# Self attention fed from the norm's fp32r parts, the gate as column tiles, the choice in two pieces, and a shifted order of units

## The chip, the cores and the metric

The kernel runs on one core of one Trainium2 chip. The metric is the device time of one execution in microseconds (us). A core has TensorE (PE, with its weight loads PEld), VectorE (DVE), ScalarE (ACT), GpSimd (POOL) and a queue, SP, that issues transfers. Each engine takes its instructions strictly in the order of the program and meets the others at semaphores.

## What is computed

Eight sequences of 512 rows and 256 columns go through three layers, each followed by a layer norm of the sum with its input:

```python
x = norm(x + linear_attention(x))      # M=128: q, k, v; state = 0.99*state + 0.01*v k^T, out = state q; then Wo
x = norm(x + cross_attention(x, ctx))  # 16 heads of 16, softmax over 512 keys
# the last layer: self attention and a mixture of experts, side by side
qkv = (x @ W_qkv + b_qkv)              # 16 heads of 16
attn_out = softmax(q k^T / 4) v
gate = softmax(x @ W_gate + b_gate)    # 8 experts
combine = the two largest gate values at their experts, 0 elsewhere   # ties go to the lower expert
moe_out = sum_e combine[e] * (x @ W_experts[e] + b_experts[e])
x = norm(x + attn_out + moe_out)
```

## The kernel before

**Slots.** The two attentions of all sequences make 16 phases (C is the cross attention of a sequence, S its self attention; from the second sequence on they alternate), and a phase has 16 slots, each for 4 heads against 128 keys. A slot has two halves, t = 2s and t = 2s + 1. In each half TensorE makes two score tiles (`sc`, waiting for the exponential of the half before) and two tiles for the row maxima of six slots ahead (`mx`, of which VectorE reduces each to one column, `maxes`). The first half also holds the product with the values of the slot before (`op`). ScalarE takes one exponential of 1024 columns from each half (`probs`).

**Units.** All other TensorE work is cut into units: projections, transposes, the gate, the experts (`moe0` to `moe15` of each sequence, six fp32r matmuls of 512 columns each), the bias of the experts (`be0`, `be1`). Tables (`LIN...`, `MID_LONG`, `MID_SHORT`, `MOE_...`) give each unit a slot and a half, relative to the start of its cross phase; `MID_LONG` serves the sequences 1 to 6. TensorE runs the units of both halves of a slot at the end of its second half, those of half 0 first. ScalarE and VectorE take a unit's result out in the half after the one of the table, so a unit of half 0 is taken out in the second half of its own slot and one of half 1 in the first half of the next, behind that half's exponential on ScalarE and behind that half's maxima on VectorE. The results of units lie alternately in two PSUM banks (`ms`), and a unit waits until the last but one before it has been taken out (`wait_unit_out(pe, *ORDER[u - 2])`).

**Names.** Every fourth slot (2, 6, 10, ... of a phase) begins its units with `shift`, a transpose of the maxima, whose result VectorE copies (`shift_r`) for a transfer into `qs`, and ends them with `heads`, which transposes the output of four finished heads. `kc0, kc1, qc0, qc1` are the two halves of the cross attention's keys and queries, `k3c0, k3c1, q3c0, q3c1` those of self attention. ScalarE writes the high fp32r part of such a unit (`high`) and VectorE the low one (`low`), which is the rest; six transfers then stack them into `ks` or `qs`. `v3a, v3b` are self attention's values, `x0, x1`, `hT0, hT1` and `x2T0, x2T1` the transposes of a norm's output or of the heads, `v1, k1, s0, s1, s23, o1, y01, y23` units of the linear attention (its v is written to `lin`). The gate's steps are `gate` on TensorE, bias and maximum on VectorE, `g_exp` on ScalarE, `choose` on VectorE (normalise, compare each pair of experts, rank, `comb`). `comb` scales the experts' results, and `combT` transposes it for `be`.

**What is fp32 here.** k3, q3, v3 and the gate multiply `x2T`, a plain fp32 copy of the transposed norm, with fp32 weights; TensorE's record shows two matmuls for each fp32 one. The experts take `x2T` and their weights as a high and a low fp32r part and make three products (high by high, low by high, high by low). ScalarE writes `x2T` and `x2T_hi`, GpSimd subtracts them to `x2T_lo` (L978), which only the experts wait for. GpSimd also adds the experts' results to `x2` and runs the norm's root.

## Time and profile before

| | |
|---|---|
| median of 3 runs | 1332.31 us (1330.14 to 1338.65) |
| the profiled execution | 1330.05 us |
| its span, first to last instruction | 1328.3 us |
| mean granted TensorE clock | 0.986 of full speed |
| TensorE busy | 1240.0 us, 93% |
| VectorE busy | 904.8 us, 68% |
| ScalarE busy | 776.4 us, 58% |
| GpSimd busy | 364.9 us, 27% |

A share of busy time is an average over the whole span. What matters for a change is the chain that sets the pace at its place. In the rows below, a time in brackets is how long the engine had stood idle before the row, and what ended that.

### The profile page before, as it was taken

What the parts mean: (1) busy time and instruction counts of PE and PEld (TensorE: products, weight loads), DVE (VectorE), ACT (ScalarE), POOL (GpSimd) and SP (SyncE); (2) the same over time, 40 slices, a digit from 0 to 9 for tenths busy, and PEclk for the clock granted to TensorE, in tenths of its full rate; (3) what the DMA queues carried; (4) which work ended last, traced back from release to release, by engine and by line L of the source; (5) the groups of instructions that cost most, each with busy time, mean ns of one, the idle gap of its engine ahead of it and who ended that gap; (6) DMA issues with size and microseconds to landing.
All of it is one profiled execution on the core that took longest, in us unless ns stands there. A gap on an engine that the chain in (4) does not pass through costs nothing.

```text
span 1328.3 us, 19317 instructions
## 1 busy us (share of the span) xinstructions
PE 1240.0 (93%) x6648; PEld 593.1 (45%) x6648; DVE 904.8 (68%) x1809; ACT 776.4 (58%) x1087; POOL 364.9 (27%) x435
## 2 busy tenths in 40 slices
PE   7888989999999999999999999999999999998995
PEld 4433445444444444444444544444444444453442
DVE  5476776567776677767776677767677777767672
ACT  2254556666566655656656665666556566666564
POOL 2310013222521224311423216122252123322162
PEclk9889999999999999999999999999999999999999
DMA  6824134304443323334422243441243333213300
GB/s 233 137 41 69 38 49 65 49 14 68 65 65 49 48 54 46 65 49 64 66 50 50 32 80 49 65 65 27 41 65 49 50 48 45 55 16 49 49 19 16
DMA packets 49840, 74.85 MB, mean 56 GB/s; under 512 B 8520, under 2 KB 20048, under 8 KB 49488
## 3 DMA queue, kind: packets, MB, share of 16 engines
q1 hardware_dynamic: 48496, 72.70, 33.8%
q10 hardware_dynamic: 1248, 0.92, 0.4%
q8 instruction: 54, 0.88, 0.3%
q14 instruction: 42, 0.34, 0.1%
HBM read 18.02 MB, written 4.19 MB: 17 GB/s over the span
## 4 chain that ended last, share of the span: by engine, by line
PE 76%; DVE 10%; issue 5%; ACT 5%; DMA 2%; SPq 1%; POOL 0%; ACTq 0%; DVEq 0%; POOLq 0%
PE ms L412 37%; PE sc L412 14%; PE op L412 14%; PE mx L412 7%; DVE maxes L831 3%; PE ms L491 2%; PE ms L436 2%; DVE k_parts L746 2%; ACT k_parts L617 1%; ACT probs L677 1%; DMA qs<-q_parts 1%; ACT x L695 1%; DMA qs<-shift_r 1%; DVE ks L915 1%; SPq L362 1%
## 5 line engine op out<-in xcount | busy, mean ns | idle before, releaser
L831 DVE TENSOR_REDUCE maxes<-mx 128x1 f32<-128x512 f32 x1024 | 657.9, 684 | 342.2 <-PE mx L412 341.2
L677 ACT ACTIVATE probs<-sc 128x1024 f32<-128x1024 f32 x512 | 524.3, 1024 | 448.6 <-PE sc L412 443.9
L993 POOL TENSOR_TENSOR x<-x,moe 128x256 f32<-128x256 f32 x256 | 187.0, 730 | 630.5 <-ACT moe L670 605.3
L412 PE MATMUL op<-probs,v 128*32 128x512 f32 x2048 | 276.0, 611 | 2.2 <-ACT probs L677 1.1
L412 PE MATMUL sc<-qs,ks 50*128 50x512 f32 x1024 | 258.1, 501 | 10.7 <-ACT probs L677 6.8
L412 PEld LDWEIGHTS sc<-qs,ks 50*128 50x128 f32 x1024 | 95.9, 184 | 322.9 <-ACT probs L677 225.7
L412 PE MATMUL mx<-ks,qs 48*128 48x512 f32 x1024 | 208.5, 403 | 13.7 <-DVE maxes L831 13.4
L670 ACT ACTIVATE moe<-ms,comb 128x256 f32<-128x256 f32 x256 | 106.7, 472 | 18.4 <-PE ms L412 18.4
L412 PEld LDWEIGHTS mx<-ks,qs 48*128 48x128 f32 x1024 | 98.4, 188 | 21.6 <-DVE maxes L831 17.4
L412 PE MATMUL ms<-we_hi,x2T_hi 128*128 128x512 f32 x256 | 94.9, 451 | 6.3 <-DVE lin L765 3.5
L412 PEld LDWEIGHTS op<-probs,v 128*32 128x32 f32 x2048 | 40.4, 108 | 95.6 <-issue 94.2
L412 PE MATMUL ms<-we_lo,x2T_hi 128*128 128x512 f32 x256 | 80.6, 396 | 0.0
L412 PE MATMUL ms<-we_hi,x2T_lo 128*128 128x512 f32 x256 | 80.5, 396 | 0.0
L412 PE MATMUL ms<-x2T,w_wqkv 128*128 128x512 f32 x128 | 61.1, 602 | 4.2 <-DVE k_parts L746 4.1
L412 PEld LDWEIGHTS ms<-we_hi,x2T_hi 128*128 128x128 f32 x256 | 39.4, 189 | 38.2 <-issue 20.3
L412 PEld LDWEIGHTS ms<-we_lo,x2T_hi 128*128 128x128 f32 x256 | 48.4, 189 | 11.4
L412 PEld LDWEIGHTS ms<-we_hi,x2T_lo 128*128 128x128 f32 x256 | 48.1, 188 | 11.5
L948 POOL TENSOR_SCALAR var<-mv 128x4 f32<-128x4 f32 x24 | 5.6, 235 | 148.5 <-DVE mv L862 147.8
L491 PEld LDWEIGHTS ms<-w_ident,oT 128*128 128x128 f32 x256 | 30.5, 141 | 24.0 <-DVE shift_r L800 16.8
L491 PE MATMUL ms<-w_ident,oT 128*128 128x128 f32 x256 | 39.2, 276 | 1.1 <-ACT oT L616 0.8
L616 ACT ACTIVATE oT<-op 128x512 f32<-128x512 f32 x64 | 38.1, 595 | 1.2 <-PE op L412 1.2
L978 POOL TENSOR_TENSOR x2T_lo<-x2T,x2T_hi 128x512 fp32r<-128x512 f32 x16 | 20.4, 1272 | 65.0 <-ACT x2T_hi L616 65.0
(107 smaller groups left out, 1193.9 us busy)
## 6 DMA issues: line engine op xcount, KB each, us to landing
ks<-k_parts SPq DMA_DIRECT2D x192, 128.0 KB, 4.5
qs<-q_parts SPq DMA_DIRECT2D x189, 128.0 KB, 5.6
xT_s<-in_xT SPq DMA_DIRECT2D x8, 512.0 KB, 4.8
x_s<-in_x SPq DMA_DIRECT2D x8, 512.0 KB, 4.4
ctxT_s<-in_ctxT SPq DMA_DIRECT2D x8, 512.0 KB, 3.9
out<-x SPq DMA_DIRECT2D x7, 512.0 KB, 2.9
qs<-shift_r SPq DMA_DIRECT2D x128, 8.0 KB
probs<-in_we SPq DMA_DIRECT2D x1, 1024.0 KB, 7.7
```

The lines of the kernel that those rows point to most:

```text
L362: sp.dma_start(dst[at:at + HD, e % RING, :, :], part[name][64 * side:64 * side + 64, which[r], :]).then_inc(stack_in[name], 16)
L412: return nc.tensor.matmul(dst, lhsT, rhs, start=first, stop=last, skip_group_check=True)
L436: last = nc.tensor.transpose(bank[:, t * P:(t + 1) * P], src[:, t, c * P:(c + 1) * P], ident[:])
L491: last = nc.tensor.transpose(bank[:, t * P:t * P + P], oT[:, t * P:t * P + P], ident[:])
L616: return nc.scalar.activation(dst, src, ACT.Copy)
L617: return nc.scalar.activation(dst, src, ACT.Identity, bias=bias, scale=1.0)
L670: nc.scalar.activation(moe[:, k % 2, j * D:j * D + D], bank[:, j * D:j * D + D], ACT.Copy, scale=comb[:, t, e:e + 1]).then_inc(moe_out, 1)
L677: nc.scalar.activation(probs[:, (2 * s + h) % 3, :, :], sc[:], ACT.Exp).then_inc(exp_out, 1)
L746: nc.vector.scalar_tensor_tensor(out=part[name][:, 1, :].bitcast(F32R), in0=unit_bank((task, n)), scalar=bias[:, c:c + 1], in1=part[name][ ...
L831: nc.vector.tensor_reduce(maxes[:, g % 2, at:at + 1], mx[:, i % 3, :], AX_X, ALU.max).then_inc(max_out, 1)
L978: nc.gpsimd.tensor_tensor(x2T_part[1][:, c, :].bitcast(F32R), x2T[:, c, :], x2T_part[0][:, c, :], ALU.subtract).then_inc(x2_low, 1)
L993: nc.gpsimd.tensor_tensor(x2[:, n % 2, t, :], x2[:, n % 2, t, :], moe[:, k % 2, j * D:j * D + D], ALU.add).then_inc(acc, 1)
```

## The change

**Self attention from parts.** `wqkv3` is no longer kept in fp32. It is loaded in two pieces into tiles that are free at the start (`heads` and half of `moe`), scaled there, and cut into `w3_part` (high on ScalarE, low on GpSimd) behind the same cut of the experts' weights. k3 and q3 become six fp32r matmuls of 512 columns, v3a and v3b twelve of 256. The fp32 copy `x2T` is gone: ScalarE writes only `x2T_hi`, and VectorE takes `x2T_lo` straight from PSUM, which then frees the bank.

**The gate as column tiles.** The gate's weight, padded to 32 columns, is now the stationary operand. Sixteen matmuls, each two records, write the four row blocks of 128 to four groups of 32 partitions; both parts of x2T pass through in fp32. ScalarE copies the result, and a new unit `gateT` transposes it back.

**The choice in two pieces.** `choose` stops after the two comparisons, and `choose_end` has the other four operations, half a slot later.

**The order.** The units of keys and values in the slots with `shift` (kc0, kc1, k3c0, k3c1, v3a) move from half 1 to half 0. hT0, hT1, x0 and x1 move about a slot later, be0 and be1 one to three slots, and moe0 to moe12 of most sequences one to two.

```diff
-LIN = {"q1": (-36, 1), "k1": (-35, 1), "v1": (-34, 1), "s0": (-27, 0), "s1": (-25, 0), "s23": (-24, 0),
-       "o1": (-23, 1), "y01": (-21, 0), "y23": (-20, 0), "x0": (-17, 0), "x1": (-16, 0), "kc0": (-14, 1),
+LIN = {"q1": (-36, 1), "k1": (-33, 1), "v1": (-32, 1), "s0": (-27, 0), "s1": (-25, 0), "s23": (-24, 0),
+       "o1": (-23, 1), "y01": (-21, 0), "y23": (-20, 0), "x0": (-16, 0), "x1": (-15, 0), "kc0": (-14, 0),
...
-MID_LONG = {"hT0": (19, 0), "hT1": (20, 0), "cy0": (21, 1), "cy1": (22, 1), "x2T0": (27, 0), "x2T1": (28, 0),
-            "gate": (29, 0), "combT": (32, 0), "be0": (33, 0), "be1": (36, 0), "k3c0": (34, 1), "q3c0": (35, 1),
+MID_LONG = {"hT0": (20, 0), "hT1": (20, 1), "cy0": (21, 1), "cy1": (22, 1), "x2T0": (27, 0), "x2T1": (28, 0),
+            "gate": (29, 0), "gateT": (31, 0), "combT": (33, 1), "be0": (36, 0), "be1": (37, 0), "k3c0": (34, 0), "q3c0": (35, 1),
...
-            "apply23": (26, 0), "g_exp": (30, 0), "choose": (30, 1)}
+            "apply23": (26, 0), "g_exp": (32, 0), "choose": (32, 1), "choose_end": (33, 0)}
...
+            def project_parts(dst, wt, src, cols):
+
+                for m, (i, j) in enumerate(((0, 0), (1, 0), (0, 1))):
+                    for c in range(DC):
+                        last = mm(dst, wt[j][:, c, cols].bitcast(F32R), src[i][:, c, :].bitcast(F32R),
+                                  m == 0 and c == 0, m == 2 and c == DC - 1)
+                return last
...
+            def project_part_rows(bank, width, src, wt, cols, blocks):
+
+                for b, t in enumerate(blocks):
+                    for m, (i, j) in enumerate(((0, 0), (1, 0), (0, 1))):
+                        for c in range(DC):
+                            last = mm(bank[:, b * width:(b + 1) * width], src[i][:, c, t * P:(t + 1) * P].bitcast(F32R),
+                                      wt[j][:, c, cols].bitcast(F32R), m == 0 and c == 0, m == 2 and c == DC - 1)
+                return last
...
+            def gate_blocks(bank, src, wt):
+
+                for i in range(2):
+                    for c in range(DC):
+                        for t in range(TB):
+                            last = mm(bank[GATE_W * t:GATE_W * t + GATE_W, 0:P], wt[:, c, :], src[i][:, c, t * P:t * P + P],
+                                      i == 0 and c == 0, i == 1 and c == DC - 1)
+                return last
...
+                elif task == "gateT":
+                    wait_unit_out(pe, "gate", n)
+                    last = nc.tensor.transpose(bank[:, 0:P], gateT, ident[:])
...
-                    copy(x2T[:, c, :], bank)
-                    copy(x2T_part[0][:, c, :].bitcast(F32R), bank).then_inc(done, 1)
+                    copy(x2T_part[0][:, int(task[3]), :].bitcast(F32R), bank).then_inc(x2_high, 1)
+                elif task == "gate":
+                    wait_unit(act, task, n)
+                    copy(gateT, bank[:, 0:P]).then_inc(done, 1)
...
                     for c in range(DC):
                         copy(we_part[0][:, c, :].bitcast(F32R), we_stage[c]).then_inc(we_cut, 1)
+                    for k in range(2):
+                        copy(w3_part[0][:, :, W3_COLS[k]].bitcast(F32R), w3_stage[k]).then_inc(w3_cut, 1)
...
+                elif task in ("x2T0", "x2T1"):
+                    c = int(task[3])
+                    dve.wait_ge(x2_high, DC * n + c + 1)
+                    nc.vector.tensor_tensor(x2T_part[1][:, c, :].bitcast(F32R), bank, x2T_part[0][:, c, :],
+                                            ALU.subtract).then_inc(x2_low, 1)
...
-                elif task in ("x2_low0", "x2_low1"):
-                    c = int(task[-1])
-                    wait_unit_out(pool, f"x2T{c}", n)
-                    nc.gpsimd.tensor_tensor(x2T_part[1][:, c, :].bitcast(F32R), x2T[:, c, :], x2T_part[0][:, c, :],
-                                            ALU.subtract).then_inc(x2_low, 1)
...
+                    pool.wait_ge(w3_cut, 2)
+                    for k in range(2):
+                        nc.gpsimd.tensor_tensor(w3_part[1][:, :, W3_COLS[k]].bitcast(F32R), w3_stage[k],
+                                                w3_part[0][:, :, W3_COLS[k]], ALU.subtract).then_inc(w3_cut, 1)
```

**TensorE, from `heads` of the slot with k3c0 to q3c0 of the next slot, sequence 2.** The `w_ident,oT` row is `heads`, `x2T,w_wqkv` is q3c0. Before:

```order
L491 MATMUL ms<-w_ident,oT 128x128 x4
L412 MATMUL sc<-qs,ks 128x512 x2
L412 MATMUL mx<-ks,qs 128x512 x2
L412 MATMUL op<-probs,v_1 32x512 x4
L412 MATMUL sc<-qs,ks 128x512 x2
L412 MATMUL mx<-ks,qs 128x512 x2
L412 MATMUL ms<-x2T,w_wqkv 128x512 x2
```

And in the changed kernel, where the `we_` rows are moe1 and the `w_hi`, `w_lo` rows q3c0:

```order
L527 MATMUL ms<-w_ident,oT 128x128 x4
L422 MATMUL sc<-qs,ks 128x512 x2
L422 MATMUL mx<-ks,qs 128x512 x2
L422 MATMUL op<-probs,v_1 32x512 x4
L422 MATMUL sc<-qs,ks 128x512 x2
L422 MATMUL mx<-ks,qs 128x512 x2
L422 MATMUL ms<-we_hi,x2T_hi 128x512 x2
L422 MATMUL ms<-we_hi,x2T_lo 128x512 x2
L422 MATMUL ms<-we_lo,x2T_hi 128x512 x2
L422 MATMUL ms<-x2T_hi,w_hi 128x512 x2
L422 MATMUL ms<-x2T_lo,w_hi 128x512 x2
L422 MATMUL ms<-x2T_hi,w_lo 128x512 x2
```

One unit, moe1, now stands between the scores of the slot and q3c0, and q3c0 is six records instead of four (each fp32 matmul makes two).

**VectorE, the maxima around k3c0, the same place.** `shift_r` is the copy of `shift`, `k_parts` the low part of k3c0, the last two rows take out `heads`. Before:

```order
L800 COPY shift_r<-ms 32x128
L831 TENSOR_REDUCE maxes<-mx 128x1 x2
L746 SCALAR_TENSOR_TENSOR k_parts<-ms,w_bk,k_parts 128x512
L807 RECIPROCAL rsum<-ms 128x16
L809 TENSOR_TENSOR heads<-ms,rsum 128x4x64
```

In the changed kernel:

```order
L848 COPY shift_r<-ms 32x128
L794 SCALAR_TENSOR_TENSOR k_parts<-ms,w_bk,k_parts 128x512
L884 TENSOR_REDUCE maxes<-mx 128x1 x2
L855 RECIPROCAL rsum<-ms 128x16
L857 TENSOR_TENSOR heads<-ms,rsum 128x4x64
```

The low part goes ahead of the next slot's first two maxima.

**VectorE, the choice of sequence 2.** `lin` is the taking out of v1, `comb` the end of the choice. Before:

```order
L800 COPY shift_r<-ms 32x128
L885 TENSOR_REDUCE g_s<-g_e 128x4
L887 RECIPROCAL g_s<-g_s 128x4
L889 TENSOR_TENSOR g_p<-g_e,g_s 128x32
L896 TENSOR_TENSOR above<-g_p 128x256
L897 TENSOR_TENSOR tied<-g_p 128x256
L900 TENSOR_TENSOR tied<-tied,w_earlier 128x256
L904 TENSOR_TENSOR above<-above,tied 128x256
L906 TENSOR_REDUCE rank<-above 128x32
L910 SCALAR_TENSOR_TENSOR comb<-rank,g_p 128x32
L831 TENSOR_REDUCE maxes<-mx 128x1 x2
L765 TENSOR_TENSOR lin<-ms,w_bv 128x512
```

In the changed kernel:

```order
L938 TENSOR_REDUCE g_s<-g_e 128x4
L940 RECIPROCAL g_s<-g_s 128x4
L942 TENSOR_TENSOR g_p<-g_e,g_s 128x32
L949 TENSOR_TENSOR above<-g_p 128x256
L950 TENSOR_TENSOR tied<-g_p 128x256
L884 TENSOR_REDUCE maxes<-mx 128x1 x2
L813 TENSOR_TENSOR lin<-ms,w_bv 128x512
L959 TENSOR_TENSOR tied<-tied,w_earlier 128x256
L963 TENSOR_TENSOR above<-above,tied 128x256
L965 TENSOR_REDUCE rank<-above 128x32
L969 SCALAR_TENSOR_TENSOR comb<-rank,g_p 128x32
```

Two maxima and the taking out of v1 now stand inside the choice, and no longer behind it; the whole lies two slots later (in slot 80 of the kernel in place of 78, with its end in slot 81).

## Rows read from the trace of the kernel before

**Rows 1.** Busy time by stretch: us, PE, PEld, DVE, ACT, POOL, PEclk, DMA, GB/s.

```profile
404.20:561.10 156.90, 150.84 (x829) 72.54 (x828) 111.28 (x226) 96.03 (x135) 45.03 (x54) 1.00 0.34 55
```

**Rows 2.** Waits of TensorE, 404.2 to 561.1 us (total, times, longest).

```profile
PE ms L436 <- DVE heads L809: 1.3, 1, 1.3
PE ms L412 <- DVE k_parts L746: 1.2, 2, 0.6
PE ms L436 <- ACT x L695: 1.0, 1, 1.0
PE ms L412 <- DVE lin L765: 0.7, 1, 0.7
PE ms L436 <- DVE k_parts L746: 0.6, 1, 0.6
PE mx L412 <- DVE maxes L831: 0.6, 1, 0.6
...
PE ms L412 <- DVE v L752: 0.3, 1, 0.3
```

**Rows 3.** Timeline of TensorE, 480.4 to 490 us (start us, us, ...).

```profile
480.46 0.40 PE L412 MATMUL mx<-ks,qs 48*128 48x512 f32 x2
...
480.78 1.06 PE L412 MATMUL op<-probs,v 128*32 128x512 f32 x8
...
481.78 0.50 PE L412 MATMUL sc<-qs,ks 50*128 50x512 f32 x2
...
482.12 0.39 PE L412 MATMUL mx<-ks,qs 48*128 48x512 f32 x2
...
482.44 1.13 PE L412 MATMUL ms<-w_be,o1T 8*128 8x256 f32 x4
...
483.49 0.73 PE L412 MATMUL ms<-we_hi,x2T_hi 128*128 128x512 f32 x2
...
485.09 0.50 PE L412 MATMUL sc<-qs,ks 50*128 50x512 f32 x2
...
486.76 0.50 PE L412 MATMUL sc<-qs,ks 50*128 50x512 f32 x2
...
487.55 1.88 PE L412 MATMUL ms<-x2T,w_wqkv 128*128 128x512 f32 x4
...
489.27 0.60 PE L491 MATMUL ms<-w_ident,oT 128*128 128x128 f32 x4
...
489.80 0.50 PE L412 MATMUL sc<-qs,ks 50*128 50x512 f32 x2
```

**Rows 4.** Timeline of all engines, 487 to 494.7 us, from `shift` to q3c0.

```profile
487.53 1.29 DVE L831 TENSOR_REDUCE maxes<-mx 128x1 f32<-128x512 f32 x2 [0.38 <-PE mx L412]
...
488.74 0.27 DVE L800 COPY shift_r<-ms 32x128 f32<-32x128 f32 x1
...
491.26 0.68 ACT L617 ACTIVATE k_parts<-ms,w_bk 128x512 fp32r<-128x512 f32 x1
...
491.98 0.75 DVE L746 SCALAR_TENSOR_TENSOR k_parts<-ms,w_bk,k_parts 128x512 fp32r<-128x512 f32 x1
...
492.78 1.98 PE L412 MATMUL ms<-x2T,w_wqkv 128*128 128x512 f32 x4 [0.59 <-DVE k_parts L746]
```

**Rows 5.** The gate in the timeline of TensorE, at 461.85 us.

```profile
461.85 1.95 PE L412 MATMUL ms<-w_wg,x2T 128*128 128x8 f32 x16
```

**Rows 6.** Instructions by line: x count, busy us, mean ns of one, idle before, releasers.

```profile
L412 PEld LDWEIGHTS ms<-we_hi,x2T_hi 128*128 128x128 f32 x256 | 39.4, 189 | 38.2 <-issue 20.3 <-DVE lin L765 5.0 <-ACT moe L670 4.8
...
L412 PE MATMUL ms<-w_wg,x2T 128*128 128x8 f32 x128 | 15.6, 257 | 0.0
```

**Rows 7.** A transfer in the chain that ended last, in order of time.

```profile
190.44 7.88 DMA qs<-q_parts
```

**Rows 8.** Timeline of the start, ScalarE and TensorE.

```profile
49.36 1.90 ACT L616 ACTIVATE we_hi<-x 128x2048 fp32r<-128x2048 f32 x1
...
52.56 1.12 PE L412 MATMUL ms<-x1T 128*128 128x512 f32 x2
```

More of the change, by code:

```diff
@@ L79 @@
+MOE_FIRST = [(26, 1), (27, 0), (28, 0), (29, 0), (30, 1), (31, 0), (32, 1), (33, 0), (33, 1), (36, 1), (37, 0),
+             (38, 0), (39, 0), (40, 0), (41, 0), (41, 1)]
+MOE_LAST_BUT_ONE = [(33, 1), (35, 0)] + [(s, 1) for s in (36, 37, 40, 41)] + [(43, 0), (44, 0)] + \
                    [(s, 1) for s in (44, 45, 46, 47, 48, 49)] + [(52, 0), (52, 1)]
[L80 removed]
+MOE_LAST = [(26, 1), (28, 0), (30, 1)] + [(s, 1) for s in range(32, 45)]
@@ L81 @@
 MOE_ENTRIES = TB * E // 2 + 2
 UNITS_LIN = ("q1", "k1", "v1", "s0", "s1", "s23", "o1", "y01", "y23", "x0", "x1", "kc0", "qc0", "cv0", "cv1", "kc1", "qc1")
-UNITS_MID = ("hT0", "hT1", "cy0", "cy1", "x2T0", "x2T1", "k3c0", "q3c0", "gate", "k3c1", "q3c1", "v3a", "v3b",
+UNITS_MID = ("hT0", "hT1", "cy0", "cy1", "x2T0", "x2T1", "k3c0", "q3c0", "gate", "gateT", "k3c1", "q3c1", "v3a", "v3b",
              "combT", "be0", "be1")
@@ L151, in own_signal @@
 def own_signal(task):
-    return task in SPLITS or task in ("be0", "be1", "shift", "heads", "gate") or task.startswith("moe")
+    return task in SPLITS or task in ("be0", "be1", "shift", "heads", "gateT", "x2T0", "x2T1") or task.startswith("moe")
 TAKEN = {unit: sum(not own_signal(ORDER[v][0]) for v in range(u % 2, u + 1, 2)) for u, unit in enumerate(ORDER)}
@@ L182, in plan_others @@
         halves["pool"][lin_at("x1_bias", n)].append(("x1_bias", 1, n))
-        for c in range(DC):
-            halves["pool"][mid_at(f"x2T{c}", n) + 2].append((f"x2_low{c}", 1, n))
         if n + 1 < B:
@@ L219, in sem @@
             return ctx.enter_context(nc.semaphore(name))
-        W = {name: sb("w_" + name, list(ap.shape)) for name, ap in w.items() if name != "we"}
+        W = {name: sb("w_" + name, list(ap.shape)) for name, ap in w.items() if name not in STAGED}
         ident = W["ident"]
@@ L236, in decoder @@
         combT = o1T[0:E, :]
+        gateT = sb("gateT", [P, P])[:]
         x1 = sb("x1", [P, TB, D])
@@ L270, in decoder @@
         we_part = (sb("we_hi", [P, DC, E * D]), sb("we_lo", [P, DC, E * D]))
+        w3_part = (sb("w3_hi", [P, DC, 3 * D]), sb("w3_lo", [P, DC, 3 * D]))
+        w3_stage = (heads[:].rearrange("p n d -> p (n d)").rearrange("p (c d) -> p c d", c=DC),
+                    moe[:, 0, :].rearrange("p (c d) -> p c d", c=DC))
+        W3_COLS = (slice(0, 2 * D), slice(2 * D, 3 * D))
         we_stage = (probs[:].rearrange("p s h t -> p (s h t)")[:, 0:E * D],
@@ L299, in decoder @@
         G_STEPS = 12
-        LATE = tuple(n for n in w if n not in FIRST + EARLY and n != "we")
+        LATE = tuple(n for n in w if n not in FIRST + EARLY + STAGED)
         block = ctx.enter_context(nc.Block())
@@ L506, in unit @@
                     wait_unit_out(pe, "x2T1", n)
+                    if n == 0:
+                        pe.wait_ge(w3_cut, 4)
                     at = (D if task[0] == "k" else 0) + c * P
-                    last = project(bank, W["wqkv3"], x2T, slice(at, at + P))
+                    last = project_parts(bank, w3_part, x2T_part, slice(at, at + P))
                 elif task in ("v3a", "v3b"):
@@ L512, in unit @@
                     wait_unit_out(pe, "x2T1", n)
-                    last = project_rows(bank, D, x2T, W["wqkv3"], slice(2 * D, 3 * D), (2 * h, 2 * h + 1))
+                    if n == 0:
+                        pe.wait_ge(w3_cut, 4)
+                    last = project_part_rows(bank, D, x2T_part, w3_part, slice(2 * D, 3 * D), (2 * h, 2 * h + 1))
                 elif task == "gate":
@@ L516, in unit @@
                     wait_unit_out(pe, "x2T1", n)
-                    last = project_rows(bank, E, x2T, W["wg"], slice(0, E), range(TB))
+                    last = gate_blocks(bank, x2T_part, W["wg"])
+                elif task == "gateT":
+                    wait_unit_out(pe, "gate", n)
+                    last = nc.tensor.transpose(bank[:, 0:P], gateT, ident[:])
                 elif task == "combT":
```

46 lines of the change are left out of this document (28 added, 18 removed), and 6 rows, old and new, of tables (LIN, MID_LONG, MID_SHORT).

## Prediction

> **What bounds the kernel now.** I read the busy time by stretch first. From about 243 us to 1181 us the kernel repeats a pattern of 32 slots; one such period takes 156.90 us [rows 1], TensorE is busy for 150.84 us of it, VectorE for 111.28, ScalarE for 96.03, and the granted clock is the full one (2.4 GHz). So TensorE sets the pace there, and two things can shorten a period: less work on TensorE, and fewer waits of it. The waits of TensorE in the same period come to 6.0 us [rows 2], each a unit that waits for its bank or its input. The timeline then gives the price list [rows 3]. The second scores of a slot start 1.67 us after the first (485.09 to 486.76), whatever the slot holds, since they wait for the exponential. After the second scores, 0.66 us pass until the first unit (481.78 to 482.44). A bias unit takes 1.05 us (to 483.49). An expert unit of six fp32r matmuls takes 1.60 us to the next scores (485.09), of which about 0.19 us is a tail that every such slot has: two experts in one slot cost 1.41 us each, 0.235 per matmul. k3c0, two fp32 matmuls in four records, takes 1.72 us (487.55 to 489.27), and `heads` with the tail 0.53. So the second half costs 0.85 us plus its units: 1.41 for an expert, 1.72 for a k3, q3 or v3 unit, about 0.35 for four small transposes.
>
> **k3 and q3.** Six fp32r matmuls of 512 columns are an expert unit's shape: 1.72 becomes 1.41, 0.31 less. Per period there are four. q3c0 and q3c1 give it all. k3c0 and k3c1 stand between `shift` and `heads`, and `heads` uses the bank of `shift`, which VectorE frees at 489.01 [rows 4], behind two maxima; the transposes then start no earlier than about 489.1 in place of 489.27 [rows 3]. There I count 0.15. Sum: 2 × 0.31 + 2 × 0.15 = 0.9 us.
>
> **v3a and v3b.** Twelve fp32r matmuls of 256 columns, each with its own load of 128 columns. The kernel has no such sequence. Bounds: the old gate is 16 records of 8 columns whose loads alone pace it, 0.113 us each (1.95 us less the last one's own 0.26, over 15) [rows 5, 6]; a weight load by itself lasts 0.189 [rows 6]. Twelve at 0.113 are 1.36 us, twelve at 0.189 are 2.27; now it is 1.72. The loads run ahead of the matmuls in the gate, and half of an expert's stream (0.235 / 2) is also 0.118, so I take a value near the low end, 0.125 or 1.50 us: 0.22 less for v3b, 0.15 for v3a (the bank of `shift` again). Sum 0.4 us; at the upper end it would be a loss of 1.1 per period. The Trainium skill ("TensorE: Matmul & The Clock Gate", "LDWEIGHTS (loading the stationary operand)") has a load take its columns over 1.2 GHz, 107 ns for 128: by that the unit is 1.28 us, and the kernel some 3 us faster than my sum; the row of 0.113 stands against so low a value.
>
> **The gate.** Its 16 records take 1.95 us to the end of the last and 1.69 to its start [rows 5, 6], which is what the slot pays beside the tail. Now there are 32 records of 128 columns in four column groups. `op` is the row nearest: eight records of 512 columns in four groups, started within 0.5 us of each other and finished within 1.06 [rows 3], so four run at a time. A quarter of the columns gives 0.107 us for each four, 0.85 in all; if issue or loads pace them as in the old gate, up to 1.7. I take 1.1, and 0.15 for `gateT`: 0.45 less, with 0 as the other bound. One rule speaks against this form: the Trainium skill ("TensorEngine Tiling (Array Packing)", "Key Properties") says that a change of tiling mode drains TensorE. The kernel changes mode in each slot, and `mx` to `op` takes 0.32 us, as does `mx` to a full-width unit [rows 3]; no drain is seen. By the rule, two more changes per sequence might cost some 0.3 us, 2.5 in all.
>
> **The waits.** This is the large term. After a unit with parts, the low part lies behind ScalarE's next exponential and VectorE's next maxima: k3c0 ends at 489.27, its high part is written from 491.26, the low part ends at 492.73, and q3c0 waits 0.59 us [rows 4]. In half 0 both are done before the next slot's maxima, and moe1 now stands before q3c0. Of the waits [rows 2] I expect these to go: hT0 on `heads` (1.3; hT0 is a slot later), q3c0 and y01 on `k_parts` (1.2), x0 on the norm (1.0; a slot later), x2T0 on `k_parts` (0.6), one on v (0.3). In all 4.4; the view starts a wait at the modelled end of the matmul before, and for q3c0 the slot has lost 0.64 where it shows 0.59, so I count 4.8. The choice holds TensorE twice in a row, at `mx` (0.6) and at moe0, which waits for v1 behind the choice (0.7). In pieces it holds nothing at `mx`, but combT now waits for its end: in that slot VectorE has two maxima (1.3), v1's 0.7 and four operations of 1.6, which end some 0.7 us after TensorE could start combT. Gain 1.3 − 0.7 = 0.6.
>
> **What it costs.** VectorE takes over x2T_lo, 2 × 0.75 us per period (the low part of k3c0 is the same form [rows 4]), on an engine that has 45 us to spare; it lies behind the maxima of its half, a slot ahead of the gate. ScalarE loses a copy. A slot left with only `shift` and `heads` cannot fall below 1.6 us in its second half: 0.3 lost. A leading low part ends at about 5.85 us after its slot's start, where the next maxima are ready at about 5.5; the scores after them need the first maximum only 0.8 us later. That slack hides it.
>
> **The sum.** Per period 0.9 + 0.4 + 0.45 + 4.8 + 0.6 − 0.3 = 6.85 us. From 243 to 1032 us there are five periods: 34 us. From 1032 to 1181 us the same units save, but no next sequence's linear attention waits: 4 us. At both ends I count nothing: before 243 us and after 1181 us the first maxima of self attention wait for the stacking of q3c0 (a transfer stands 7.88 us on the chain at 190.44 [rows 7]); what is saved before it is mostly waited for, and one or two experts move from in front of that wait to behind it. The start loses: ScalarE cuts 2048 weights per row in 1.90 us, now 1536 more (1.5 us), ahead of the copies of q1 and k1, for which s0 starts at 52.56 with nothing to spare [rows 8]: 1.3 us. In all 34 + 4 − 1.3 = 36.7, from the profiled 1330.05 us to 1293. That execution lies 2 us below the median of the runs, so 1294 for a median.
>
> **Rivals.** (a) The sum as above, chance 0.60: 1281 to 1304. (b) v3's loads are not hidden: twelve at 0.189, 1.5 us per period more than I count, in eight sequences 12 us: 1306; chance 0.08. For it: nothing here shows a 256-column fp32r matmul. Against: the old gate's loads. (c) The waits only move. Each unit waits for the unit two before it, and there is hardly a slot in which something isn't moved; if half of the 4.8 comes back at other units, six times, 14 us: 1308; chance 0.2. For it: x2T_lo and the low parts are one after another on VectorE. (d) The change of order brings nothing, so that only the cheaper units count: 1.75 × 6 − 1.3 = 9 us, 1321; chance 0.07. (e) The other side: VectorE stands in its order behind the high part. It waits from the copy of `shift` (about 4.0 us into the slot) to the end of ScalarE's part (5.1), and meanwhile no maximum is taken. There are about 30 leading units in the repeating part. If a high part came later by 0.5 us or more, `mx` would wait; it decides at 0.8 us each (24 us, then the change is worth less than 1%), and from 1.7 us each, 50 us, it is slower: 1345. Against it: VectorE is idle for 45 us a period, and only one part comes per slot. Chance 0.05, half of it above 1345.
>
> **The numbers.** 1294, the median by (a). The range goes from the low ends of v3 and the gate with a few more waits gone, 1279, to (c) and a little beyond, 1313. About 1% (13 us) is what a measurement of this kernel can tell from no change. Faster by more means below 1319: (a), (b), (c) and half of (d), 0.92; within 1%: 0.055; slower 0.025.
>
> **What the profile will show.** A stretch of 32 slots at about 150 us in place of 156.90; k3 units of six records 0.235 us apart; v3 records 0.12 to 0.13 apart; the gate within 1.3 us; no wait on `k_parts` or on the norm's x; a wait of about 0.7 at combT; the start later by about 1.3 us. I am wrong if v3's records are spaced over 0.15 us, if `mx` waits for maxima in the slot after a leading unit, or if new waits at moe units add up to over 2 us per period.

## The result and the profile after

| | before | after |
|---|---|---|
| median of the runs | 1331.22 us (1327.26 to 1338.65, 4 runs) | 1293.26 us (1290.36 to 1295.98, 4 runs) |
| ratio | | 0.9706, 95% interval 0.9673 to 0.9738 |
| the profiled execution | 1330.05 us | 1295.17 us |
| its span | 1328.3 us | 1293.4 us |
| mean granted TensorE clock | 0.986 | 0.981 |
| TensorE busy | 1240.0 us | 1224.4 us, 95% |
| VectorE busy | 904.8 us | 911.8 us, 70% |
| ScalarE busy | 776.4 us | 776.9 us, 60% |
| GpSimd busy | 364.9 us | 348.4 us, 27% |

The kernel is 2.9% faster: 38.0 us between the medians, 34.9 us between the two profiled executions. I locate the gain by the starts of the first scores of a slot. Below, a slot's "second half" is the time from its second scores to the next slot's first ones.

| us from slot to slot | slot 0 begins | 0 to 34 | 34 to 66 | 66 to 98 | 98 to 194 | 194 to 226 | 226 to 255 |
|---|---|---|---|---|---|---|---|
| before | 73.15 | 170.08 | 160.95 | 156.93 | 470.80 | 149.00 | 132.18 |
| after | 73.69 | 172.79 | 154.26 | 150.27 | 450.71 | 144.56 | 131.89 |
| gain | -0.54 | -2.71 | 6.69 | 6.66 | 20.09 | 4.44 | 0.29 |

So five stretches of 32 slots gain 6.7 us each, the stretch with no further linear attention gains 4.4, and 3.3 us are lost before slot 34. The busy times of one period of the changed kernel, columns as in [rows 1]:

```profile
400.74:551.01 150.27, 148.77 (x862) 73.77 (x861) 112.07 (x229) 96.00 (x134) 42.49 (x52) 1.00 0.34 58
```

Against [rows 1] TensorE does 2.1 us less and idles 1.5 us where it idled 6.1: two thirds of a period's gain is time in which TensorE stood waiting. The view of waits in the same period has these left for TensorE (total, times, longest):

```profile
PE sc L422 <- ACT probs L721: 0.5, 2, 0.2
...
PE ms L422 <- DVE x1b L835: 0.3, 1, 0.3
PE ms L564 <- DVE comb L969: 0.3, 1, 0.3
...
PE ms L422 <- ACT o1T L659: 0.2, 1, 0.2
```

Every row of [rows 2] is gone: there is no wait on `k_parts`, on the norm's `x`, on `heads`, on `lin` or on `maxes`. The next fence is the timeline of the changed kernel in that period, in the form of [rows 3, 4]: the gate in slot 77, the end of the choice and combT in slot 81, k3c0 in slot 82, q3c0 in slot 83, v3a in slot 86.

```profile
458.04 0.64 PE L422 MATMUL ms<-x2T_hi,w_wg 128*32 128x128 f32 x16
458.50 0.62 PE L422 MATMUL ms<-x2T_lo,w_wg 128*32 128x128 f32 x16
459.05 0.51 PE L422 MATMUL sc<-qs,ks 50*128 50x512 f32 x2
...
475.25 0.19 DVE L969 SCALAR_TENSOR_TENSOR comb<-rank,g_p 128x32 f32<-128x32 f32 x1
...
475.59 0.60 PE L564 MATMUL ms<-w_ident,comb 128*8 128x128 f32 x4 [0.28 <-DVE comb L969]
...
478.92 0.73 PE L422 MATMUL ms<-x2T_hi,w_hi 128*128 128x512 f32 x2 [0.16 <-ACT o1T L659]
479.49 0.63 PE L422 MATMUL ms<-x2T_lo,w_hi 128*128 128x512 f32 x2
...
479.96 0.63 PE L422 MATMUL ms<-x2T_hi,w_lo 128*128 128x512 f32 x2
...
480.68 0.69 ACT L660 ACTIVATE k_parts<-ms,w_bk 128x512 fp32r<-128x512 f32 x1 [0.91 <-PE ms L422]
...
481.40 0.75 DVE L794 SCALAR_TENSOR_TENSOR k_parts<-ms,w_bk,k_parts 128x512 fp32r<-128x512 f32 x1 [1.38 <-ACT k_parts L660]
...
482.07 1.28 DVE L884 TENSOR_REDUCE maxes<-mx 128x1 f32<-128x512 f32 x2
...
484.79 0.63 PE L422 MATMUL ms<-x2T_hi,w_hi 128*128 128x512 f32 x2
...
499.80 0.40 PE L422 MATMUL ms<-w_hi,x2T_lo 128*128 128x256 f32 x2
500.04 0.40 PE L422 MATMUL ms<-w_lo,x2T_hi 128*128 128x256 f32 x2
```

The gate's 32 records and the tail of the slot lie between 458.04 and 459.05. k3c0's second and third pair start 0.47 us apart, 0.235 a record, and v3a's pairs of 256 columns 0.24 apart, 0.12 a record. Before, the low part of k3c0 ended at 492.73, 2.93 us into the next slot, which began at 489.80 [rows 3, 4]; now it ends at 482.15, 1.20 us into the next slot, which begins at 480.95. q3c0 at 484.79 has no bracket: it waits for nothing. VectorE pays for it: it stands 1.38 us behind the high part.

**Where the 2.7 us before slot 34 went.** Slot 22 of the first sequence takes 9.05 us in place of 6.96. Its k3c0 needs both low parts of x2T, and the second one stands behind a maximum on VectorE. The timeline of the changed kernel at that place:

```profile
179.63 1.27 DVE L884 TENSOR_REDUCE maxes<-mx 128x1 f32<-128x512 f32 x2
...
180.83 0.68 DVE L864 TENSOR_TENSOR x2T_lo<-ms,x2T_hi 128x512 fp32r<-128x512 f32 x1
181.43 1.27 DVE L884 TENSOR_REDUCE maxes<-mx 128x1 f32<-128x512 f32 x2
181.76 0.71 PE L422 MATMUL ms<-x2T_hi,w_hi 128*128 128x512 f32 x2 [0.68 <-DVE x2T_lo L864]
...
182.84 1.06 PE L422 MATMUL ms<-x2T_hi,w_lo 128*128 128x512 f32 x2
```

and its busy times by stretch there, with the granted clock third from the end:

```profile
180.00:184.00 4.00, 2.96 (x10) 2.13 (x11) 2.89 (x6) 0.89 (x2) 0.00 (x0) 0.83 0.02 4
184.00:188.00 4.00, 4.00 (x22) 2.41 (x21) 1.27 (x2) 1.43 (x2) 0.00 (x0) 0.74 0.24 68
```

After the wait the same pair of records lasts 1.06 us in place of 0.63, with the granted clock at 0.74 in the mean, between the two levels. The slot has two waits that the kernel before doesn't have there: 0.54 us of `mx` for the maxima, then 0.68 of k3c0. In the repeating part a whole slot lies between x2T and the gate, and nothing waits for `x2T_lo`.

How much of the 2.1 us in slot 22 is the wait, and how much the clock? Eight of the kernels below also have the changed kernel's first sequence. Five of them (parts_only, no_lead, early_transposes, q_leads, comb_later) show slot 22 at 7.95 us, with the same two waits and the full clock; in two (parts_late_comb, w3_later) it takes 9.05 as here; in one_choice the clock fell a slot earlier. So the waits are worth about 1.0 us against the slot of before (more, since its units have become cheaper), and the fall of the clock behind them 1.1 us, which comes in some executions only. The rest of the stretch: slots 23 to 26, in the last of which the first maxima of self attention wait for the stacking of q3c0, take 20.5 us in place of 18.7, again 0.7 of it where the clock fell (slot 26: 8.85 us, 8.1 to 8.2 in those five kernels); slots 1 and 2 are 1.7 longer and slot 12 is 1.5 shorter, which the same kernels show either way; and the cheaper units from slot 27 on give 1.2 back.

### The profile page after: what moved, and what is told of

It is laid out like the page before. It is cut to its first block, busy times and chain, and to the rows that moved or that the text cites. A ratio compares the mean times of both kernels' runs of the same rounds, so it can differ in the third digit from the quotient of the medians.

```text
span 1293.4 us, 19863 instructions
## 1 busy us (share of the span) xinstructions
PE 1224.4 (95%) x6912; PEld 603.1 (47%) x6912; DVE 911.8 (70%) x1825; ACT 776.9 (60%) x1081; POOL 348.4 (27%) x421
## 4 chain that ended last, share of the span: by engine, by line
PE 78%; DVE 9%; ACT 5%; issue 4%; DMA 2%; SPq 1%; POOL 0%; ACTq 0%; DVEq 0%
PE ms L422 36%; PE op L422 15%; PE sc L422 15%; PE mx L422 8%; DVE maxes L884 4%; ACT probs L721 2%; PE ms L527 2%; DMA qs<-q_parts 2%; PE ms L472 1%; ACT moe L714 1%; DVE ks L974 1%; SPq L370 1%; PE ms L522 1%; DVE x1b L835 1%; DMA qs<-shift_r 1%
## 5 line engine op out<-in xcount | busy, mean ns | idle before, releaser
L794 DVE SCALAR_TENSOR_TENSOR k_parts<-ms,w_bk,k_parts 128x512 fp32r<-128x512 f32 x32 | 24.0, 751 | 39.2 <-ACT k_parts L660 38.7
L660 ACT ACTIVATE k_parts<-ms,w_bk 128x512 fp32r<-128x512 f32 x32 | 22.0, 687 | 28.8 <-PE ms L422 28.8
```

Source lines behind the costliest of these rows:

```text
L660: return nc.scalar.activation(dst, src, ACT.Identity, bias=bias, scale=1.0)
L794: nc.vector.scalar_tensor_tensor(out=part[name][:, 1, :].bitcast(F32R), in0=unit_bank((task, n)), scalar=bias[:, c:c + 1], in1=part[name][ ...
```

## Experiments

### One half of the change at a time

**order_only** has before's arithmetic with the new tables, without gateT and with the choice in one piece:

```diff
-"gate": (29, 0), "combT": (32, 0), "be0": (33, 0), "be1": (36, 0), "k3c0": (34, 1)
+"gate": (29, 0), "combT": (33, 1), "be0": (36, 0), "be1": (37, 0), "k3c0": (34, 0)
...
-"g_exp": (30, 0), "choose": (30, 1)}
+"g_exp": (32, 0), "choose": (32, 1)}
```

> The kernel before with the changed kernel's order of units and nothing else: fp32 k3, q3, v3 and gate (no gateT, the choice in one piece, at the changed place). Theory A (most of the gain is waits that the order removes): per period of 32 slots 5.1 us of the 6.7 that the changed kernel gains, so a period near 151.8 us and a whole of about 1303 us. Theory B (the waits vanish only because the units became shorter, and the order adds little): a period above 154.5 us, 1317 us or more.

Measured: 1323.51 us (1318.77 to 1327.62), ratio 0.9926 (0.9899 to 0.9952). The period came out near the expected one, 152.86 for 151.8 us, but the whole is 20 us above the 1303 expected: what the periods give is largely lost at both ends (see below). **parts_only** is its counterpart: the new arithmetic with before's tables for the sequences 1 to 6, where gateT and the choice had to find a place:

```diff
-"gate": (29, 0)
+"gate": (29, 0), "gateT": (30, 0)
...
-"g_exp": (30, 0), "choose": (30, 1)}
+"g_exp": (31, 0), "choose": (31, 1), "choose_end": (31, 1)}
```

> The changed kernel with the old order for sequences 1 to 6 (LIN, LIN_THIRD, MID_LONG and the experts' tables of before; gateT at slot 30, g_exp and the whole choice at slot 31). Theory A: 1.7 us per period from the cheaper units, less what the later choice costs at moe0, so 155 to 156.5 us a period and 1322 to 1328 us. Theory B: most of the gain is here, below 1310 us.

Measured: 1333.31 us (1328.11 to 1336.76), ratio 1.0003 (0.9975 to 1.0031): no gain, where 5 to 11 us were expected. The starts of slots for these two, and for the experiments below:

| us | slot 0 begins | 0 to 34 | 34 to 66 | 66 to 98 | 98 to 130 | 194 to 226 | 226 to 255 |
|---|---|---|---|---|---|---|---|
| before | 73.15 | 170.08 | 160.95 | 156.93 | 156.93 | 149.00 | 132.18 |
| after | 73.69 | 172.79 | 154.26 | 150.27 | 150.22 | 144.56 | 131.89 |
| order_only | 71.16 | 177.22 | 156.84 | 152.86 | 152.86 | 151.22 | 137.22 |
| parts_only | 72.93 | 170.85 | 163.89 | 158.50 | 156.95 | 146.81 | 132.55 |
| parts_late_comb | 73.05 | 172.70 | 162.40 | 156.94 | 156.93 | 148.36 | 133.34 |
| no_lead | 73.98 | 170.95 | 157.09 | 153.11 | 153.09 | 147.46 | 133.93 |
| early_transposes | 78.34 | 169.81 | 155.71 | 151.70 | 151.69 | 145.35 | 134.08 |
| one_choice | 75.30 | 169.98 | 154.84 | 150.90 | 150.90 | 147.49 | 131.82 |
| q_leads | 72.81 | 170.89 | 156.83 | 151.00 | 150.94 | 145.74 | 133.52 |
| comb_later | 72.52 | 170.98 | 154.98 | 150.96 | 151.03 | 145.31 | 132.59 |
| x2T1_leads | 73.84 | 170.66 | 154.20 | 150.26 | 150.23 | 144.63 | 133.42 |
| w3_later | 71.44 | 171.99 | 154.24 | 150.20 | 150.19 | 144.66 | 133.04 |
| order_mid | 74.59 | 170.30 | 157.02 | 152.86 | 154.42 | 150.21 | 134.69 |

Slot 0 begins between 71 and 75 us in kernels that are the same up to there (once at 78), so differences of that column alone tell nothing.

A period is 156.93 with neither half, 152.86 with the order alone (152.2 if the choice in one piece costs what it does below), 156.95 with the parts alone, 150.24 with both. The two halves don't add up: with the order in place the parts give 2.6 us, without it nothing. parts_only shows why. Its cheaper units are there: against before the second halves of slots 77, 82, 83, 86, 87, 90 and 91 are shorter by 0.78, 0.15, 0.32, 0.15, 0.32, 0.15 and 0.31 us. Slot 79, where moe0 waited for v1, is shorter by 1.20. But with gateT between `shift` and v1 in slot 78, v1 falls to the bank of `shift`, which VectorE hasn't emptied, and the choice comes in one piece of nine operations. TensorE in its timeline, slots 78 and 80:

```profile
470.70 0.27 PE L559 MATMUL ms<-w_ident,gateT 128*128 128x128 f32 x1
472.22 2.05 PE L421 MATMUL ms<-w_wv,xT_s 128*128 128x128 f32 x16 [1.24 <-DVE shift_r L847]
...
480.62 0.51 PE L421 MATMUL sc<-qs,ks 50*128 50x512 f32 x2
482.70 0.76 PE L421 MATMUL mx<-ks,qs 48*128 48x512 f32 x2 [1.57 <-DVE maxes L883]
483.39 1.01 PE L563 MATMUL ms<-w_ident,comb 128*8 128x128 f32 x4
484.06 1.20 PE L421 MATMUL ms<-we_hi,x2T_hi 128*128 128x512 f32 x2
```

Slot 78 is 1.62 longer than before's, slot 80 longer by 1.84 at full clock and by 3.36 in this period, where the clock fell behind the wait (the pair of experts lasts 1.20 in place of 0.73 us). **parts_late_comb** moves combT and be0 out of that wait's way:

```diff
-"combT": (32, 0), "be0": (33, 0), "be1": (36, 0)
+"combT": (33, 0), "be0": (35, 0), "be1": (36, 0)
```

> The kernel of parts_only (cheaper units, the old order), in which combT waited 3.4 us for the choice, with combT a slot later and be0 two slots later in the long sequences, so that this wait has room. If the cheaper units are worth what the sum took (1.75 us per period) and moe0's old wait of 1.2 is gone as it was there, less 1.3 for gateT in a slot with shift: about 155 us per period and 1318 us. If the order, not the units, carries the gain, this stays far above 1293; if the two only work together for another reason, it stays near 1333.

Measured: 1336.28 us (1333.36 to 1345.56), ratio 1.0039 (1.0018 to 1.0059). The expectation was wrong: the wait only passed from combT to moe1 (slot 80 alone with moe1 has a second half of 4.13 us, where one expert needs 2.27), and slot 78 is as it was. The loss sits at the choice and at gateT's place, not at combT. Other places for gateT or a choice in two pieces within the old order were not tried, so that the cheaper units bring nothing is shown for these places only; k3, q3 and v3 gave their full 1.4 us a period even here.

### The moves one by one, taken back from the changed kernel

**no_lead** puts the units with `shift` back behind the next maxima:

```diff
-"kc0": (-14, 0)
+"kc0": (-14, 1)
...
-"kc1": (-6, 0)
+"kc1": (-6, 1)
...
-"k3c0": (34, 0)
+"k3c0": (34, 1)
...
-"v3a": (38, 0)
+"v3a": (38, 1)
...
-"k3c1": (42, 0)
+"k3c1": (42, 1)
```

> The changed kernel with kc0, kc1, k3c0, k3c1 and v3a of the repeating part back in half 1; TensorE's order is the same, only the taking out comes half a slot later. Theory A: the next unit waits again for the low part: 0.64 at qc0, about 0.5 at x2T0, 0.6 at moe1, 0.4 at s1, 0.65 at y01, 2.8 us per period, 15 us in all, about 1308 us. Rival (VectorE standing behind the high part costs as much as the lead brings): within 3 us of the changed kernel's 1293.

Measured: 1313.20 us (1312.33 to 1315.06), ratio 0.9853 (0.9791 to 0.9915). A period is 2.84 us longer, at the five units that follow a part: slots 67, 75, 83, 87 and 91 have 3.24, 3.87, 4.31, 3.32 and 3.80 us in place of 2.58, 3.33, 3.67, 2.94 and 3.13. In its timeline the wait of [rows 4] is back, now at moe1, which stands ahead of q3c0:

```profile
486.32 0.73 PE L422 MATMUL ms<-we_hi,x2T_hi 128*128 128x512 f32 x2 [0.58 <-DVE k_parts L794]
```

So the expert before q3c0 does not cover the wait, it takes it over: it is the lead that removes it. (The lead without that expert was not run.) The rest lies outside the periods, 2.9 us of it from slot 194 to 226, where the same units follow each other.

**early_transposes** puts hT0, hT1, x0 and x1 a slot earlier:

```diff
-"x0": (-16, 0), "x1": (-15, 0)
+"x0": (-17, 0), "x1": (-16, 0)
...
-"hT0": (20, 0), "hT1": (20, 1)
+"hT0": (19, 0), "hT1": (20, 0)
```

> The changed kernel with x0, x1 and hT0, hT1 a slot earlier again (as before), everything else as changed. Theory A: x0 waits about 1.0 us for the norm and hT0 about 1.3 us for heads, once per period each: 2.3 us less what the slots they leave then save (nothing), 13 us in all, about 1306 us. Rival (the faster slots have moved the norm and the heads early enough): no wait, 1293 us.

Measured: 1304.01 us (1300.41 to 1307.10), ratio 0.9779 (0.9725 to 0.9833). A period is 1.46 us longer, not 2.3. Slot 67 with hT0 and qc0 has 3.78 and slot 68 gives 0.44 back: 0.76 for the wait on `heads`. Slot 95 has 3.72 and slot 97 gives 0.39 back: 0.75 for the wait on `x`. Its view of waits tells why this is less than the 2.3 of [rows 2]:

```profile
PE ms L472 <- ACT x L739: 1.0, 1, 1.0
PE ms L472 <- DVE heads L857: 0.8, 1, 0.8
```

The wait on `heads` had been 1.3; the lead of kc0 has already taken 0.5 of it. The one on `x` is as long as before, but in the changed kernel the next slot's first scores wait 0.2 us for their exponential there, which is a part of the same time.

**one_choice** joins the choice again in the place of its first piece:

```diff
-"choose_end": (33, 0)}
+"choose_end": (32, 1)}
```

> The changed kernel with the whole choice in one piece at slot 80 (second half). Theory A (the two pieces let two maxima and v1 pass between them): mx of slot 81 then waits about 1.0 us behind the choice and combT no longer waits for its end but for v1: 0.6 to 1.0 us more per period, 1296 to 1299 us. Rival (the place of the choice, not its cut, is what counts): 1293.

Measured: 1302.22 us (1300.01 to 1303.77), ratio 0.9775 (0.9746 to 0.9804). A period is 0.65 us longer, all of it in slot 81 (3.81 in place of 3.15), as expected: 3.2 us in five periods. The stretch from slot 194 to 226 loses 2.9 more, all of it in slot 209 (8.01 in place of 5.11), where the choice stands for the last sequence but one: `mx` waits 1.87 us there for the maxima in place of 0.27, and the granted clock falls behind it. The profiled execution (1300.01) is 4.8 us above the changed kernel's; the 9 us between the medians go beyond that since it was the fastest of its four runs and the changed kernel's profiled one was 1.9 above its median. So the 6.1 us of these six stretches are what the cut accounts for.

### Going further

**q_leads** lets the queries' units lead too:

```diff
-"qc0": (-13, 1)
+"qc0": (-13, 0)
...
-"qc1": (-5, 1)
+"qc1": (-5, 0)
...
-"q3c0": (35, 1)
+"q3c0": (35, 0)
...
-"q3c1": (43, 1)
+"q3c1": (43, 0)
```

> The changed kernel with qc0, qc1, q3c0 and q3c1 of the repeating part in half 0 as well. No heads unit follows them, so their high part ends only 0.7 us after the slot, and VectorE stands in its order behind it. Theory (the lead pays only where heads covers it): the next maxima come about 0.7 us late, mx and the exponential each wait 0.1 to 0.2 us, four times per period, against 0.25 won at q1 and 0.3 at moe11: 0.2 to 0.7 us more per period, 1294 to 1297. Rival (a lead always pays): 0.5 us less per period, 1290.

Measured: 1300.22 us (1299.45 to 1301.84), ratio 0.9762 (0.9729 to 0.9795). Worse by 0.7 us a period, the upper end of what was expected (the total is above it): nothing waits for these parts early, while the slots after them (68, 76, 84) wait 0.16 for their exponential, which now stands behind the high part on ScalarE, and slot 84 loses 0.23 more. A lead pays only where the next unit needs the bank.

**comb_later** takes combT away from the end of the choice, where the changed kernel still waits:

```diff
-"combT": (33, 1)
+"combT": (35, 0)
```

> The changed kernel with combT two slots later for the sequences 1 to 6: from the end of slot 81 to slot 83 (sequence 2), ahead of moe1. In the changed kernel combT waits for the end of the choice (about 0.7 us in slot 81), and its copy on ScalarE then stands ahead of slot 82's parts (0.28 us more there than its units cost). If these two are losses of their own, slot 81's second half falls from 3.15 to about 2.3 us, slot 82's from 3.17 to 2.9, slot 83's rises from 3.67 to 4.0 for the transposes: 0.8 us per period, 5 to 6 periods, 1288 to 1289 us. If the slots are held by something else at the same time (the expert's results, the bank), the waits reappear at moe0, k3c0 or be0 and the time stays at 1293.

Measured: 1298.35 us (1297.09 to 1301.30), ratio 0.9732 (0.9703 to 0.9762): slower by 5 us, where 4 us less were expected. The second half of slot 81 did fall, to 2.27 us, and that of slot 82 to 2.89; a period grew by 0.7 all the same. The timeline shows both new waits:

```profile
473.05 1.28 DVE L884 TENSOR_REDUCE maxes<-mx 128x1 f32<-128x512 f32 x2
...
473.88 0.49 PE L422 MATMUL mx<-ks,qs 48*128 48x512 f32 x2 [0.44 <-DVE maxes L884]
...
482.01 0.60 PE L564 MATMUL ms<-w_ident,comb 128*8 128x128 f32 x4
...
483.10 0.73 PE L422 MATMUL ms<-x2T_hi,w_hi 128*128 128x512 f32 x2 [0.49 <-ACT moe L714]
```

With slot 81 shorter, VectorE is not through with the choice and the maxima behind it when slot 82's `mx` is due, and its first half has 2.37 us in place of 1.66. In slot 83, q3c0 now wants the bank of moe1, which ScalarE has just begun to empty: 4.85 us in place of 3.67, of which the transposes are some 0.35. combT's wait was cover for VectorE.

**x2T1_leads** moves x2T1 of the first and last sequence half a slot ahead of k3c0's slot:

```diff
-"x2T1": (21, 1)
+"x2T1": (21, 0)
```

> The changed kernel with x2T1 in half 0 for sequences 0 and 7, the two in which k3c0 comes in the next slot. In the changed kernel k3c0 of sequence 0 waits 0.68 us more by the trace for x2T_lo on VectorE (181.76), the granted clock falls for the rest of the slot, and the slot takes 9.05 us in place of 6.96. Theory (the late low part causes both): k3c0 does not wait, the clock stays, that slot is back at about 6.7 us, and q3c0's stack and the maxima of self attention come 2 us earlier: 1290 to 1291. Rival (the fall of the clock has another cause, or the gain is lost again at the transfer): 1293.

Measured: 1294.72 us (1294.24 to 1296.34), ratio 0.9722 (0.9698 to 0.9747): no difference from the changed kernel, where 2 to 3 us less were expected. k3c0 no longer waits, but slot 22 takes 7.63 us and not the 6.7 expected: VectorE now has both low parts ahead of its maxima, and `mx` waits for these.

```profile
179.20 1.27 DVE L864 TENSOR_TENSOR x2T_lo<-ms,x2T_hi 128x512 fp32r<-128x512 f32 x2
...
180.40 2.55 DVE L884 TENSOR_REDUCE maxes<-mx 128x1 f32<-128x512 f32 x4
181.13 0.49 PE L422 MATMUL mx<-ks,qs 48*128 48x512 f32 x2 [1.07 <-DVE maxes L884]
```

So it is VectorE's work in this slot, not the place of one low part, that costs the time; the move is worth 0.3 us against the 7.95 of the kernels in which the clock doesn't fall. Slots 0 to 34 take 170.66, but kernels with x2T1 in its old place come to 170.9 as well: 1.9 us of the 2.7 lost there are of the execution, not of the kernel.

**w3_later** cuts the self attention's weights two slots later, behind the copies of q1 and k1:

```diff
                         copy(we_part[0][:, c, :].bitcast(F32R), we_stage[c]).then_inc(we_cut, 1)
+                if t == 2 * -10:
                     for k in range(2):
                         copy(w3_part[0][:, :, W3_COLS[k]].bitcast(F32R), w3_stage[k]).then_inc(w3_cut, 1)
```

> The changed kernel with the high cut of the self attention's weights two slots later, so that ScalarE writes the copies of q1 and k1 before it. If the cut is what delays the start, the first scores of slot 0 come about 0.5 us earlier (72.9 to 73.2 us in place of 73.69) and the time is 1292.5; if the start does not hang on it, or the cut now delays a later copy by as much, it stays at 1293.

Measured: 1293.21 us (1292.23 to 1295.77), ratio 0.9697 (0.9667 to 0.9726). The cause is confirmed in the timeline. After first:

```profile
46.38 0.69 ACT L660 ACTIVATE q_parts<-ms,bq2s 128x512 fp32r<-128x512 f32 x1 [3.86 <-DMA qs<-q_parts]
...
50.56 1.04 ACT L659 ACTIVATE w_hi<-heads 128x1024 fp32r<-128x1024 f32 x1
51.51 0.62 ACT L659 ACTIVATE w_hi<-moe 128x512 fp32r<-128x512 f32 x1
52.03 0.67 ACT L660 ACTIVATE x1T<-ms,w_bq 128x512 f32<-128x512 f32 x1
...
53.43 2.04 PE L422 MATMUL ms<-x1T 128*128 128x512 f32 x2 [1.39 <-ACT x1T L660]
```

and w3_later:

```profile
46.57 0.69 ACT L660 ACTIVATE q_parts<-ms,bq2s 128x512 fp32r<-128x512 f32 x1 [3.87 <-DMA qs<-q_parts]
...
50.76 0.68 ACT L660 ACTIVATE x1T<-ms,w_bq 128x512 f32<-128x512 f32 x1
...
51.90 1.06 ACT L659 ACTIVATE w_hi<-heads 128x1024 fp32r<-128x1024 f32 x1
...
52.16 1.12 PE L422 MATMUL ms<-x1T 128*128 128x512 f32 x2
```

s0 follows `q_parts` after 7.05 us with the cut ahead and after 5.59 with it behind: 1.46 us. That is within the scatter of the whole kernel, and neither version is measurably the better (1292.5 us were expected).

### The ends of order_only

order_only loses 7.1 us before slot 34, 2.2 from slot 194 to 226 and 5.0 after slot 226. **order_mid** gives the first and last sequence their old gate, choice and experts back:

```diff
-             "k3c0": (22, 0), "q3c0": (22, 1), "gate": (23, 0), "k3c1": (27, 1), "q3c1": (28, 1), "v3a": (29, 1),
+             "k3c0": (22, 0), "q3c0": (22, 1), "gate": (24, 0), "k3c1": (27, 1), "q3c1": (28, 1), "v3a": (29, 1),
...
-MOE_LAST = [(26, 1), (28, 0), (30, 1)] + [(s, 1) for s in range(32, 45)]
+MOE_LAST = [(s, 1) for s in (25, 26, 30)] + [(s, 1) for s in range(32, 45)]
```

> The new order with the arithmetic of before (as order_only), but the first and the last sequence keep their old places of the gate, the choice and the experts. order_only gained about 4 us in each repeating period, yet lost some 10 us before slot 34 and after slot 226, where TensorE stood waiting and its granted clock was low. If the later experts of the first and last sequence cause that loss (nothing is left to do while q3c0 is stacked), slot 34 begins near 243 us again, the tail takes 132 us, and the time is about 1314. If the loss comes from the other moves, it stays at 1322.

Measured: 1322.39 us (1315.75 to 1323.41), ratio 0.9899 (0.9859 to 0.9938). The cause was right for the beginning (170.30), half right for the tail (134.69), and yet the total barely moved, since two of the middle periods were longer than 152.86 in this execution: 154.42, and 157.10 from slot 162 to 194. (order_only has one such period too, 154.13 us from slot 130 to 162.) The busy times by stretch in the longer one show the granted clock:

```profile
915.00:920.00 5.00, 4.98 (x27) 2.10 (x27) 3.08 (x6) 4.18 (x7) 1.28 (x1) 1.00 0.78 122
...
923.00:926.00 3.00, 3.00 (x16) 1.12 (x9) 1.27 (x3) 1.01 (x2) 0.00 (x0) 0.50 0.00 0
```

and TensorE's timeline where it fell:

```profile
918.66 0.50 PE L413 MATMUL sc<-qs,ks 50*128 50x512 f32 x2
...
919.33 1.95 PE L413 MATMUL ms<-w_wg,x2T 128*128 128x8 f32 x16
921.21 0.80 PE L413 MATMUL sc<-qs,ks 50*128 50x512 f32 x2
```

The clock falls as the old gate ends, 1.95 us of small matmuls, with TensorE never idle around it. TensorE then runs at the lower of its levels (1.2 GHz) for some 10 us, and the period loses 4.2. In other periods of the same kernel the same place keeps the full clock (152.86). I counted the slot behind the gate of the six sequences 1 to 6 (slots 46, 78, 110, 142, 174, 206) in every profiled execution. With the old gate in the new order it is longer than 3.29 us in six cases of twelve (4.56 and 4.14 in order_only; 4.81, 4.82, 5.34 and 4.49 in order_mid), each time with a fall of the granted clock. With the column-tiled gate in the new order it is 3.27 to 3.29 in all 48 cases of eight kernels. In the kernel before, where k1 shares the old gate's slot and v1 follows, the five repeating ones are alike (4.77). So part of what the cheap gate gives in the new order is most likely that this fall doesn't come; whether the gate's shape is the cause was not tried by itself.

## Why the prediction was right, step by step

The forecast was 1294 us, the median 1293.26; the sum was 36.7 us, the profiled executions differ by 34.9. Since order_only and the changed kernel have the same tables but for gateT and the choice, the second halves of their slots price each arithmetic term by itself.

| term, per period | predicted | measured | from |
|---|---|---|---|
| k3, q3 | 0.90 | 1.10 | slots 82, 83, 90, 91: 3.49, 3.99, 3.04, 3.44 to 3.17, 3.67, 2.89, 3.13 |
| v3 | 0.40 | 0.46 | slots 86, 87: 3.05, 3.23 to 2.88, 2.94 |
| gate with gateT | 0.45 | 0.46 | slots 77, 79: 2.55, 2.58 to 1.68, 2.99 |
| choice, less combT's wait | 0.60 | 1.06 | slot 79 of before, 3.86 where one expert needs 2.27; slot 81 of after, 3.15 where combT and an expert need 2.61 |
| waits gone, less the floor | 4.50 | 3.65 | 156.93 to 152.86, order_only, is 4.07; 0.42 of it belongs to the choice (slot 81: 3.78 for 2.61) |
| sum | 6.85 | 6.7 | |

**k3 and q3.** 0.235 us a record, as taken from the expert. k3c1 gave 0.15, as counted for a unit between `shift` and `heads`. k3c0 gave 0.32: it starts late (it waits for o1T), and by its end the bank of `shift` has been free for a while, so nothing holds `heads`. That it starts late is a cost of its own, told under the waits.

**v3.** 0.12 us a record: the upper bound of 0.189 and with it rival (b) fell. By the rule of the Trainium skill ("TensorE: Matmul & The Clock Gate", "LDWEIGHTS (loading the stationary operand)") such a load is estimated at 107 ns; the trace has about 0.12 us from record to record, whatever bounds it.

**The gate.** The total was right by luck, by two errors that cancel. The 32 records cost 0.83 us over an empty slot (1.68 less the 0.85 of a second half), not 1.1: the lower bound, a quarter of the columns each, was the truth. gateT cost 0.41 us in slot 79 and not 0.15. The Trainium skill's rule that a change of tiling mode drains TensorE ("TensorEngine Tiling (Array Packing)", "Key Properties") has nothing here to show it: the unit ends at its bound with a change on either side.

**The choice.** Counted too low. I took what it cost before from the view of waits, 0.6 and 0.7 us; the slot had lost 1.59. What is left at combT was taken at 0.7; its bracket shows 0.28, the slot loses 0.54. Of the 1.06 us gained, 0.42 come from the later place and the rest, 0.64, from the cut (one_choice: 0.65). What the prediction did not see is what the wait at combT covers (comb_later).

**The waits.** This step came out 0.85 too high, and the choice hides 0.46 of that in the sum. All of [rows 2] went, as forecast: 4.3 us by the slots (1.3 at hT0, 0.5, 0.65, 0.4 and 0.65 at the parts, 0.75 at x0), which no_lead (2.84) and early_transposes (1.46) give too. I had counted 4.8, because one slot, q3c0's, had lost 0.05 more than its row shows, and I raised all rows for it; and x0's 1.0 was worth 0.75. Most of the rest is a wait that I took at nothing: k3c0 now follows combT and waits for ScalarE to empty that bank (0.16 by its bracket, 0.45 over its form of before in order_only's slot 82, 0.28 in the changed kernel).

**The periods and the ends.** Five periods gave 33.4 us for 34, the stretch after slot 194 gave 4.4 for 4. The start was right in mechanism and size: the cut costs 1.46 us by w3_later, 1.3 was counted; the 0.54 at slot 0 is less mostly because that execution was 0.6 us ahead at `q_parts`. Wrong was "at both ends I count nothing": slots 0 to 34 lost 2.7 us. I had costed x2T_lo on VectorE where a slot lies between it and its reader, and not in the first sequence, where k3c0 follows at once. About 0.8 of it is of the kernel (170.9 us in kernels that are alike there, against 170.1), the rest of this execution's clock. So the total has luck in it: the ends lost 2 us more than the 1.3 counted for the start, the choice and the gate's bound gave back what the waits and gateT took.

**The rivals.** (c), new waits, came to about 0.6 us a period (slots 82 and 95, 0.3 each over their units), far from its 2.4. (d), the order bringing nothing, is the opposite of what was found: by parts_only it is the parts that bring nothing in the old order. No rival had that, and the sum of separate terms could not show it. (e) is real in its mechanism and has no price here: VectorE stands 1.38 us behind k3c0's high part, the next maxima begin 0.4 us after they could, and `mx` doesn't wait once in the period. comb_later and x2T1_leads show how near it is: a slot shorter by 0.87 us, or another low part ahead of the maxima, and `mx` waits 0.44 or 1.07 us. In q_leads the loss comes by way of ScalarE instead, at the exponential.
